# Three stations of a pipelined two-layer decoder divided in two, late halves in other banks, orders written anew

## Chip, cores and metric

One core of a Trainium2 chip runs the kernel. The metric is the device time in microseconds (us), the median of several executions; lower is better. Engines are named as in the profile: PE is TensorE (PEld its weight loads), DVE is VectorE, ACT is ScalarE, POOL is GpSimd, SP is SyncE, whose queue issues every DMA.

## What is computed

Two decoder layers on 32 sequences of 128 rows and 256 channels. Each of the six sublayers is added to its input and normalized over the channels:

```python
x = layernorm(x + L0_attn(x))            # 16 heads, window of 7 rows, learned window weights
x = layernorm(x + L0_xattn(x, ctx))      # cross attention, one head, additive mask
x = layernorm(x + L0_ffn(x))             # 8 experts, each attends over its 16 best rows of a sequence
x = layernorm(x + L1_attn(x))            # attention with a decay mask
x = layernorm(x + L1_xattn(x, ctx))      # argmax picks one context row each; 16 heads over them
x = layernorm(x + L1_ffn(x))             # w1, depthwise conv over rows, silu, w2; ternary weights, int8-like rows
```

## The kernel before, in words

The 32 sequences form 16 groups of two (NG = 16, 256 rows each). A group passes eight **stations**, which are Python generators on each engine: Q queries and A windowed (first attention), B cross (cross attention), X experts, C decayed (decay attention), D choose and E memory (the argmax attention), F feed_forward. S is the setup of weights. A station yields after each step. `ORDER` holds one string for each engine; `walk` reads it letter by letter, and each letter issues the next step of that station on that engine, so the whole interleaving of the groups is written out by hand. While group 15 is in A, group 13 or so is in C and group 11 in F. An engine works strictly in its own order; between engines there are only semaphores.

A step is named here by station, group and number on its engine, counted from 0: PE's C4.5 is the sixth step of C for group 4. The numbering of the undivided station is used for both kernels.

PSUM has eight banks. Station Q and A share bank_a, X has bank_x, F has bank_f, E has the four banks_e, and B, C and D share bank_c. Each PE step fills a bank, ACT or DVE empties it, and the next PE step of the station waits for that: a round trip, which other stations' PE steps have to cover. The stations' PE steps are: X 0 to 5 routing, gather and the experts' projection, X 6 to 12 rotation transposed, scores, softmax, values, projection back; E 0 to 8 scores, maxima, logits, exponentials, values, for two sequences in turn, E 9 and 10 turning the heads and projecting with wc1x; F 0 to 5 quantization rows and the four w1 products, F 6 to 8 the second row scale and the w2 product.

Between two sublayers stands the norm. DVE adds the bank to x (`norm`, L932, instruction at L934, one instruction and one accumulator read for each of the two sequences), ACT squares and sums (`squares`, L1386), POOL works out scale and shift (L1674 to L1680), ACT applies them (`normed`, L1397). The semaphore `added` was raised once, after both sequences:

```python
for b in range(GB):
    last = dve.scalar_tensor_tensor(x[:, b, :], bank[b], ..., accum_out=n.sums[:, b:b + 1])
last.then_inc(n.added, 1)
```

In F, DVE and ACT alternate for each of four pairs of channel blocks (jj): DVE empties the w1 product (`evacuated`, L1310), ACT starts the convolution (`middle`, L1642), DVE adds its two shifted taps (`convolved`, L1319), ACT takes the tanh (L1647), DVE multiplies (`gated`, L1329), ACT takes the magnitude (L1651), DVE keeps the largest (`largest`, L1335). After that come the maximum over channels, a second scale (L1355 to L1361), the scaled copies (L1365), and the w2 product. On DVE the loop was, for every group: largest(at - 3), gated(at - 2), convolved(at - 1), evacuated(at).

Of the kernel before, what the change touches and what calls it, by code (L numbers as in the profile page):

```python
# [11 lines left out]
ALU = mybir.AluOpType  # L12
# [3 lines left out]
P = 128  # L16
# [46 lines left out]

UNIT16 = 2.0 ** 24
# [5 lines left out]
        "QQQASSASASSQBQBAQAADSBABASBBQBQBXXASAXQXAXBXBAAXBBXQBXQXXBXAXAXQCXCABXXBXABAXBQXCXQCXXXBXCAXCAXBXQDAXDXD"  # L70
        "XDADXEABBXXEBQCEBEQEXCXECEXCXECECEXDAXEDADQDAFXDFDFAEBXFBEXBFXBEXEBFBXACXEQCECECXQECFXCXEXDEFXDEXDFDAXAD"
        "FDQEFXBFEBXFBXFBEXEFABCEAXABEXCQCECXQXCECEXFDXFEXEDFXDADFADXDQEFBFXEFBABXEBXFXBFEBAXEACXCEQCXEXCQECFXCXE"
        "DXEFXDAEDXDFDADQEFXBFEFBFXBAXBEFEFXACECAXBBXECQCEXQXCEXFCXEFXEDEXFDXADDFADFDFQEXBFAEBXFBXBXEFBEBAACEXCEX"
        "CQXEXCFEDXCEXCFXEQXEFDXADADFQDFDAEFXBEBXFBXBEXFBEBFACEAXECXQCQCXEXCFXCXDXEXFEDAEDEDFDADXQEFBFEFXBXABFBXB"
        "FXCEFEABXEXCAECQXCXEXFQCXECEFXEDXAEDFDXDADDFEFBFEFXBXBQBFXABEXEBFACEXCAXECECXQXCFECEXDFEXQDXDXAEDFDXDAEF"
        "QBXFEFBFBXBFEXEXFBABAEACXECXQCQECXFXECXECXEXDXAFEDADXDFDQDAEFXBFEFBFXBABXFBEBEXFEACEXQXCECXCXEXCEXECXDFX"
        "EFDQXADFDADXFDQEBFEFBXFBABEFXEXBFBEXCAACEXCECXFXDECXFCEXBEXEDXFDXDFADAFDFXEXBEFBXBFEXBEBFXCXECXECXECXFXC"
        "FECEXEDXEFDXDDFFDFDXFXECXCECFCXECFCEDXEXEDXEXFDXFEXDXDEDEFECECECFFFECEFCCFDFEEDEDEDFEDEFDEFEEFFFEEFEFEFE"
        "EEFEFEFFFFFFFFFFFFF"
    ),  # L80
    "DVE": (
        "QSQSSQQASSSSSASSSASSSSSSSSSAASSSAAASSAAAAAAAAAAAAAAAQQQQSSSSSSSSSSSSASSSSSSSSSAAASSSSSSSBBAASSSSSAAABAAA"
        "AAAAAAAAAAAAQXSSXXXXXXXXAXXQQQAAAXBBXXAAAAABXXAAAAAAAAAAAAAAAQQQQXAAXXXXXXXXXAXAXBBAAAAAXXBXAAAAAAXXAAAC"
        "ACAAAAAQQQQXCAAXXXXXXXXXAXAXDDDXEXXAAEBBXXEEAEEEEAABAAAAAAAAAAAAEEQAAQQQCCAEECXEAAFFFDDDAXAXXXFXXXXEXEFF"
        "FXFEEFXEEEEFFBBFFFXXXBAAFFAAAXFFXFFAAAEEAFAACCFAFAAAFFFCEEAAAAFFFXAQEFQQQFDDDFFFXAXXXAXXXXXEXEFXEEFFFEEE"
        "EFFFFBBFFFFAAXXFXFABEEAFAAAFFXAXAAFAAACCAAFFAACEEFFFAAQFFFFXAEQQQFAAFFFDDDAAXXXXXXXXXEEFXXEEEEEAEFFFBBFF"
        "FFAFXXXFFBFAAXXFFFEEFAAAAAAAAFFCCFAAFAAAACFEEFFAAAXAFFFQEFQQXQDDDXFXXXAXXXXFFFAEEXXEFEFFEEEEFFAFFFBBAFFF"
        "FFXXXFFAAFBAFEAAFXXEAAACCFFAAAAAAAACFFFEEFFFXFAAEAAFQXQQQFFFXDDDXXXAXXXXFAFFEEFAFXEFFFEFEEBBEEXFFFABXXXF"
        "AAFAAAFEFXXFEAAAFAAFFCCFFFAAAAEEAACAAXFFFFAAEQFQQQFFFXADDDXXXXXXXXAAAEEFXXEEFFEEEFFEBBFFFXXXBFFFAFAEFFEX"
        "AAAFFAAAXFFCCFFAAAAACFFFAAAAXAAAEEFFFFQQQEDDDQFAFFFXAXXXEXEXXXXEFXXEFFFFBBEEEAFFFEFFFFAXXXFBFFXFXAAFAAAF"  # L90
        "EEFFAAAACCAAAAFFFAAAACEEAAXAFFFFEQQQFQDDDXFFFXXXXAXXXEEAFXEXXFFFEFEEEBEBFFFAAFFFXXBFXFFFFAFAXEXEFAAAAAAC"
        "CFFAAAFFFCEEAAAAAAAAFFFAXFQQQQEDDDFXXXXXFFFAEEXXXXAXXEFEFFFEEEEBFBFFFFFFFAABXXXAAFFFEFAAAFFEXXFFAAAAAAAC"
        "CFAAAFFAAAEEACAQXQQFFFEFQAAXXXDDDXFFFFXXXXXAAEEXXEFEFFFFBBFEEEEFFFBFFFXXAXAFFFEEFXFFXAAAAAAAFFCCAAAAEEAA"
        "CAAXAFFFAAFFFEFXXXXXXXXQXQFDDDFFFAQQAXXEEEFEFFEEEEFFBBFFFAAFFFXXFXBFFFFAAFAAAEEAAAFXXFCFCAFFFAAAAAACEEFF"
        "FFAAXAAEAFFXFFXDDDXXXXXXAXFXXEEFFEEFFEEEEBBFFFXXXBFFFFXXFFFFEEFFFFCCFFFFFFCEEFXEFXXXXXFFFXDDDXXXFXXFFEFE"
        "FFFEEFEECEECFFFFFFCXXXFFFFXXEEFFFFFFFFFDDDXEEFEEEFFFEEEEEEFCCFFFFFCFFFFFFEEFFFFFFFFDDDFEEFFFFFFEFEEFFFEE"
        "EEEEFFFFFFFFEEFFFFFFFFFFFFEEFFFFFFFEFFFFFFFFFFFFFFFFFFFFFFFFFFFFFFFF"
    ),
# [14 lines left out]
    "POOL": (
        "ABBABBXXABBXCXCABXBCCXEABBXCFCXEFABBXCCFXEFABBXCCFXEFABBXCCXFEFABBXCFCXEFABBXCCFXEFABBXCFCXEFABBXCFCXEFA"
        "BBXCFCXEAFBBXCCXFEFABBXFCCXEFABBXCFCXEFCCXFXFECCFEFFEFFF"
# [47 lines left out]
def build(nc, io, out):  # L163
    ctx = ExitStack()
    with ctx:
# [53 lines left out]
        _, carve = area("area_a", 8216)  # L219
# [54 lines left out]
        am_f, sc1_f, rs1_f, rs2_f = (carve(GB) for _ in range(4))  # L274

# [29 lines left out]
        x_in = [next(sems(f"x_in{i}")) for i in range(2)]  # L305

# [46 lines left out]
        I = w["ident"][:, :]  # L353

# [17 lines left out]
        def _(sp):  # L372
# [77 lines left out]
            def feed_forward(g):  # L450
                sp.wait_ge(n_f.done, g + 1)
                sp.dma_start(out[g * T:(g + 1) * T, :].rearrange("(b t) d -> t b d", b=GB),
                             xs[g % NX][:, :, :]).then_inc(y_out, 16)
                yield
# [7 lines left out]
        def _(pe):  # L462
# [99 lines left out]
            def windowed(g):  # L562
# [33 lines left out]
                until("a", n_a.added, g + 1)  # L596
                yield

            def cross(g):
# [35 lines left out]
                until("c", n_b.added, g + 1)  # L635
                yield

            def experts(g):
                x = xs[g % NX]
                if g:  # L640
                    pe.wait_ge(n_x.added, g)
# [25 lines left out]
                for j in range(EJ):  # L667
# [9 lines left out]
                    yield  # L677
                pe.wait_ge(x_rot, g + 1)
                qkv3 = blocks(qkv_x, EJ)
                for j in range(EJ):  # L680
                    for i in range(2):
                        at = 2 * j + i
                        last = pe.transpose(bank_x[:, at * P:(at + 1) * P], qkv3[:, j, i * HP:(i + 1) * HP], I)
# [1137 lines left out]
```

## Time and profile before

| what | us |
|---|---|
| device time, median of 3 executions (lowest, highest) | 1035.07 (1033.67, 1036.02) |
| device time of the profiled execution | 1034.66 |
| its span in the profile | 1032.9 |
| PE busy | 915.1 (89% of the span) |
| DVE busy | 864.8 (84%) |
| ACT busy | 744.9 (72%) |
| POOL busy | 205.5 (20%) |

The span is what the views are made of; the device time of the same execution is 1.8 us longer. The profile lists for each instruction its start, its length and what ended the idle time before it. PE's mean granted clock over the span is 0.97 of full speed.

### The profile page before, as it was taken

The numbers are of one execution on the slowest core, as the hardware profiler recorded it, in microseconds if no ns is written. First come the engines' busy times: TensorE is split into PE (matmuls) and PEld (weight loads), VectorE is DVE, ScalarE is ACT, GpSimd is POOL, SyncE is SP. The second block draws the span as 40 slices with busy tenths as digits, with TensorE's granted clock in tenths as the row PEclk, the third lists the DMA queues.
The fourth block names the chain that finished last, engine by engine and source line by source line (L and its number), as shares of the span: only waits on it lengthen the run. The fifth ranks groups of instructions, "written<-read, shape, count | busy, mean of one in ns | idle before, by whom it ended". The sixth has DMA issues, their size and how long they took to land.

```text
span 1032.9 us, 20266 instructions
## 1 busy us (share of the span) xinstructions
PE 915.1 (89%) x7382; PEld 666.8 (65%) x7382; DVE 864.8 (84%) x2216; ACT 744.9 (72%) x1857; POOL 205.5 (20%) x469
## 2 busy tenths in 40 slices
PE   6778998999999999999999999999999988897552
PEld 4566666767676776767775767768676756574331
DVE  4987668599898999899999999998999886868755
ACT  2375565777877878787878788777968787867643
POOL 2011221213131211313131312213131312110010
PEclk9989999999999999999999999999999999999765
DMA  8932221110303030211203030302102000000000
GB/s 269 370 80 82 71 61 32 46 47 22 92 1 113 1 112 1 71 42 52 62 11 102 1 92 22 110 3 68 46 31 72 22 1 21 2 22 2 11 10 11
DMA packets 36628, 59.06 MB, mean 57 GB/s; under 512 B 6656, under 2 KB 15872, under 8 KB 36016
## 3 DMA queue, kind: packets, MB, share of 16 engines
q1 hardware_dynamic: 36528, 57.76, 18.1%
q8 instruction: 59, 0.97, 0.4%
q14 instruction: 41, 0.34, 0.1%
HBM read 28.77 MB, written 4.19 MB: 32 GB/s over the span
## 4 chain that ended last, share of the span: by engine, by line
PE 54%; ACT 17%; DVE 16%; SPq 6%; issue 4%; POOL 3%; DMA 1%; ACTq 0%; POOLq 0%; DVEq 0%
PE bank_c L465 16%; PE banks_e L465 8%; PE bank_a L465 7%; PE bank_x L465 6%; DVE area_f L1319 4%; PE bank_f L465 3%; ACT area_e L1608 3%; DVE neg_top L1259 3%; ACT squares_out L1393 3%; SPq L435 2%; PE banks_e L843 2%; ACT area_f L1642 2%; PE bank_a L571 2%; PE bank_x L674 2%; DVE x L934 1%
## 5 line engine op out<-in xcount | busy, mean ns | idle before, releaser
L1319 DVE SCALAR_TENSOR_TENSOR area_f<-area_f,w_convw 128x254 f32<-128x254 f32 x256 | 111.7, 478 | 9.7 <-ACT area_f L1642 7.7
L1381 ACT ACTIVATE area_bx<-bank_x 128x512 f32<-128x512 f32 (+1 forms) x144 | 70.2, 499 | 22.3 <-PE bank_x L674 7.5
L1057 DVE TENSOR_TENSOR area_a<-area_a 128x512 f32<-128x512 f32 x112 | 73.0, 684 | 14.2 <-ACT area_a L1381 12.5
L1259 DVE TENSOR_REDUCE neg_top<-banks_e 128x8 f32<-128x1024 f32 x64 | 76.4, 1219 | 10.1 <-PE banks_e L465 9.9
L1642 ACT ACTIVATE area_f<-area_f,w_convb,w_convw 128x256 f32<-128x256 f32 x128 | 69.8, 595 | 17.8 <-DVE area_f L1310 17.6
L1608 ACT ACTIVATE area_e<-banks_e 128x512 f32<-128x512 f32 x128 | 69.1, 598 | 10.2 <-PE banks_e L843 10.1
L1112 DVE TENSOR_TENSOR area_a<-area_a 128x512 f32<-128x512 f32 x112 | 74.9, 684 | 1.7
L1116 DVE TENSOR_TENSOR area_a<-area_a 128x512 f32<-128x512 f32 x96 | 65.7, 684 | 0.3
L1381 ACT ACTIVATE area_a<-bank_a 128x512 f32<-128x512 f32 (+1 forms) x80 | 44.2, 552 | 26.2 <-PE bank_a L465 21.0
L1381 ACT ACTIVATE area_bx<-bank_c 128x512 f32<-128x512 f32 x64 | 34.7, 542 | 33.7 <-PE bank_c L465 26.3
L465 PE MATMUL bank_x<-area_bx 128*128 128x128 f32 (+1 forms) x256 | 51.6, 334 | 4.1 <-ACT area_bx L1381 3.1
L1688 POOL TENSOR_TENSOR area_bx<-area_bx,minus 128x2 f32<-128x2 f32 x16 | 11.8, 740 | 197.9 <-ACT area_bx L1405 197.9
L1310 DVE TENSOR_TENSOR area_f<-bank_f,area_f 128x512 f32<-128x512 f32 x64 | 43.8, 684 | 7.3 <-PE bank_f L465 6.9
L1647 ACT ACTIVATE area_f<-area_f 128x512 f32<-128x512 f32 x64 | 40.4, 631 | 12.8 <-DVE area_f L1319 12.5
L465 PE MATMUL bank_f<-area_f,w1q 128*128 128x256 f16 x256 | 41.3, 287 | 9.3 <-DVE area_f L1310 7.1
L465 PEld LDWEIGHTS bank_x<-area_bx 128*128 128x128 f32 x256 | 40.7, 190 | 12.8 <-ACT area_bx L1381 6.2
L674 PE MATMUL bank_x<-w_wqkv_e,area_bx 128*32 128x384 f32 x512 | 47.9, 492 | 0.0
L1329 DVE SCALAR_TENSOR_TENSOR area_f<-area_f 128x512 f32<-128x512 f32 x64 | 43.9, 685 | 3.0 <-ACT area_f L1647 2.0
L1381 ACT ACTIVATE area_e<-banks_e 128x256 bf16<-128x256 f32 (+1 forms) x64 | 34.6, 541 | 16.0 <-PE banks_e L496 8.2
L1365 DVE TENSOR_TENSOR area_f<-area_f,bank_f 128x512 f16<-128x512 f32 x64 | 40.2, 681 | 5.3 <-PE bank_f L866 5.2
L465 PE MATMUL banks_e<-chosen_key,chosen_q 32*128 32x256 f32 x512 | 37.6, 408 | 6.6 <-DVE neg_top L1259 4.5
L465 PE MATMUL banks_e<-area_e,chosen_v 128*32 128x512 f32 x256 | 35.3, 618 | 8.6 <-ACT area_e L1608 8.6
(318 smaller groups left out, 2575.1 us busy)
## 6 DMA issues: line engine op xcount, KB each, us to landing
area_a<-area_a SPq DMA_DIRECT2D x96, 224.0 KB
area_a<-in_xT SPq DMA_DIRECT2D x16, 256.0 KB, 2.9
area_bx<-in_ctxT SPq DMA_DIRECT2D x16, 256.0 KB, 3.0
x<-in_x SPq DMA_DIRECT2D x16, 256.0 KB, 3.6
area_d<-in_ctxT SPq DMA_DIRECT2D x16, 256.0 KB, 2.7
y<-x SPq DMA_DIRECT2D x16, 256.0 KB, 2.2
w_wqkv_e<-in_wqkv_e SPq DMA_DIRECT2D x1, 3072.0 KB, 11.2
area_f<-in_raw SPq DMA_DIRECT2D x2, 1024.0 KB, 12.2
```

Source lines behind the costliest of these rows:

```text
L465: last = pe.matmul(out_ap, l, r, start=i == 0 and not opened, stop=closes and i == len(pairs) - 1)
L674: last = pe.matmul(bank_x[ES * q:ES * (q + 1), 0:3 * HP], xgf[:, c, e, :], wq[:, c, e, :], start=c == 0, stop=c == DC - 1)
L1057: return dve.tensor_tensor(product_of(wi).rearrange("p (n t) -> p n t", t=P), qT0.rearrange("p c (b t) -> p (c b) t", t=P), kT0.rearrange( ...
L1112: made[wi] = own.mark(dve.tensor_tensor(v4, v4, bc(e4[:, :, wi, :], 3, DH), ALU.mult))
L1116: added = dve.tensor_tensor(vw[:, to, :], vw[:, to, :], vw[:, wi, :], ALU.add)
L1259: dve.tensor_reduce(top[:, b, r:r + 2, :, 0].rearrange("p r (par c) -> p r c par", c=DC), banks_e[:, r:r + 2, :].rearrange("p r (c par k) ...
L1310: dve.tensor_tensor(blocks(th_f[jj % 3], 2), blocks(bank_f[:, :], 2), bc(tscale_f, 1, 2), ALU.mult).then_inc(f_h, 1)
L1319: last = dve.scalar_tensor_tensor(c4[:, i, :, dst], h4[:, i, :, src], cwt3[:, 2 * jj + i, k:k + 1], c4[:, i, :, dst], ALU.mult, ALU.add)
L1329: dve.scalar_tensor_tensor(c_f[jj], th_f[jj % 3], 1.0, c_f[jj], ALU.add, ALU.mult).then_inc(f_silu, 1)
L1381: return act.activation(dst, src, ACT.Copy)
L1608: act.activation(pT_e[:, r * 4 * P:(r + 1) * 4 * P], bank_e[r][:, :], ACT.Exp, scale=float(DH) ** -0.5).then_inc(e_exp, 1)
L1642: last = act.activation(c4[:, i], h4[:, i], ACT.Identity, bias=w["convb"][:, j:j + 1], scale=cwt3[:, j, 1:2])
```

## The change

**Stations.** X becomes X (steps 0 to 5 on PE) and Y `combine` (6 to 12); E becomes E (0 to 8) and T `connect` (9 and 10); F becomes F (0 to 5) and H `gate` (6 to 8). The other engines' steps are divided in the same places. The work of a group is the same. A second half may now stand in a string behind first steps of the next group's first half.

**Banks.** With `LATE = 13`:

```diff
+        def joined(g):
+            return (bank_a, bank_a) if LATE <= g < NG - 1 else (bank_e[0], bank_e[2])
+        def upper(g):
+            return bank_a if g == NG - 2 else bank_x
+        def gating(g):
+            return gate_late if g == NG - 2 else gate_f
+        def rear(g):
+            return bank_x if LATE <= g < NG - 1 else bank_f
```

So T of groups 13 and 14 uses bank_a, Y of group 14 bank_a, H of groups 13 and 14 bank_x, and F of group 14 has its own buffers (in the area of A, which is done by then). PE's waits follow, among them:

```diff
             def memory(g):
...
+                elif g <= LATE:
+                    pe.wait_ge(n_e.added, GB * g)
                 else:
-                    pe.wait_ge(n_e.added, g)
+                    pe.wait_ge(e_att, 2 * g)
...
             def feed_forward(g):
...
-                if g:
-                    pe.wait_ge(n_f.added, g)
+                if g > LATE:
+                    pe.wait_ge(f_h, NJ * g)
+                elif g:
+                    pe.wait_ge(n_f.added, GB * g)
```

The w2 product of group 15 goes to bank_a and bank_x instead of bank_a and bank_c.

**Norm.** `added` is raised for each sequence, and ACT's squares wait for their own:

```diff
                 for b in range(GB):
-                    last = dve.scalar_tensor_tensor(x[:, b, :], bank[b], ...)
-                last.then_inc(n.added, 1)
+                    dve.scalar_tensor_tensor(x[:, b, :], bank[b], ...).then_inc(n.added, 1)
...
-                act.wait_ge(n.added, g + 1)
                 for b in range(GB):
+                    act.wait_ge(n.added, GB * g + b + 1)
```

**Last group.** Of the last norm ACT applies one sequence and DVE the other; the last store waits for both:

```diff
+                if g == NG - 1:
+                    dve.wait_ge(n_f.scaled, n_f.steps * NG)
+                    dve.tensor_scalar(x[:, 1, :], x[:, 1, :], n_f.scale[:, 0, 1:2], n_f.scale[:, 1, 1:2],
+                                      ALU.mult, ALU.add).then_inc(last_normed, 1)
```

In F of group 15 the loops turn round: DVE takes evacuated(at), convolved(at - 1), gated(at - 2), largest(at - 3), and ACT

```diff
-                for at in range(NJ + 3):
-                    for lag, step in ((3, magnitude), (2, tanh), (1, middle)):
+                lags = ((0, middle), (2, magnitude), (1, tanh)) if g == NG - 1 else ((3, magnitude), (2, tanh), (1, middle))
```

**Orders.** The strings of PE, DVE, ACT and POOL are written anew, SP's is the same. The last of PE's characters, before and after:

```diff
-...EEDEDEDFEDEFDEFEEFFFEEFEFEFEEEFEFEFFFFFFFFFFFFF
+...DEDEDEDHETDHDTHEEFFFEEFEFEFEEEHTHTHFFFFFFHHHHHH
```

and of ACT's:

```diff
-...EFFFFEFEEEEFFEFFFFEEFFEEFFEFEEFEFFFFFFFFFFFFFFFFFF
+...HFFFHEFEEEEFFFEFFFEEFFEEFFEFTTTFFFFFFFFFFFFFFFHHHH
```

As another place, the steps between C4.5 and D4.1. On PE:

```diff
-C4.5 X5.11 E3.8 D4.0 X5.12 E3.9 F2.7 X6.0 D4.1
+C4.5 X5.11 D4.0 E3.8 X5.12 D4.1
```

and on ACT, around the squares C4.5 and the norm C4.6 (X5.10 is the pair at L1542, X5.9 a copy of bank_x):

```diff
-C4.4 X5.9 X5.10 C4.5 D4.0 C4.6
+C4.4 E3.10 X5.9 C4.5 X5.10 D4.0 C4.6
```

At the start of DVE's string S0.0 to S0.2 now stand before Q0.0, and X0.0 to X0.8 before Q2.0.

## Rows read from the trace of the kernel before

**Rows 1.** Windows: us, busy us per engine (instructions), granted clock, DMA share, GB/s.

```profile
231.00:770.00 539.00, 517.64 (x4331) 386.02 (x4331) 495.84 (x1279) 424.26 (x1078) 125.30 (x272) 1.00 0.16 50
770.00:950.00 180.00, 158.39 (x1375) 112.94 (x1373) 144.74 (x369) 144.16 (x357) 32.39 (x79) 1.00 0.08 23
...
960.00:988.00 28.00, 17.67 (x136) 8.88 (x136) 21.27 (x46) 17.58 (x35) 0.76 (x3) 0.69 0.03 10
...
1000.00:1033.00 33.00, 8.85 (x36) 4.50 (x36) 18.60 (x39) 11.71 (x23) 1.55 (x5) 0.55 0.03 9
```

**Rows 2.** Waits of PE, 231 to 950 us: total us, times, longest.

```profile
PE bank_x L465 <- ACT area_bx L1381: 3.6, 7, 1.4
...
PE bank_c L496 <- ACT x L1400: 0.9, 2, 0.6
```

**Rows 3.** Timeline of PE, last stretch: start, us, instruction, idle before.

```profile
917.16 1.89 PE L465 MATMUL banks_e<-w_wc1x,area_e 128*128 128x256 f32 x8
...
920.01 1.15 PE L465 MATMUL banks_e<-chosen_key,chosen_q 32*128 32x256 f32 x16 [0.53 <-DVE x L934]
...
960.75 2.09 PE L465 MATMUL banks_e<-chosen_key,chosen_q 32*128 32x256 f32 x16 [2.54 <-DVE neg_top L1259]
...
988.35 3.40 PE L465 MATMUL banks_e<-w_wc1x,area_e 128*128 128x256 f32 x8
...
1002.30 1.04 PE L465 MATMUL bank_f<-area_f,w1q 128*128 128x256 f16 x4 [0.79 <-DVE area_f L1310]
```

**Rows 4.** Timeline of POOL at the hand-over from memory attention to feed-forward.

```profile
994.89 0.20 POOL L1680 TENSOR_TENSOR bn_scale_e<-bn_negmean_e,bn_scale_e 128x2 f32<-128x2 f32 x1
```

**Rows 5.** Timeline of ACT, the same hand-over and the end.

```profile
996.01 0.58 ACT L1400 ACTIVATE x<-x,bn_scale_e 128x256 f32<-128x256 f32 x1
...
997.97 0.89 ACT L1625 ACTIVATE area_f<-x,area_f 128x256 f16<-128x256 f32 x2
...
1026.76 0.51 ACT L1393 ACTIVATE squares_out<-x,bn_sums_f 128x256 bf16<-128x256 f32 x1 [8.86 <-DVE x L934]
...
1029.72 0.58 ACT L1400 ACTIVATE x<-x,bn_scale_f 128x256 f32<-128x256 f32 x1
```

**Rows 6.** Timeline of DVE, last group.

```profile
991.79 0.42 DVE L934 SCALAR_TENSOR_TENSOR x<-banks_e,x 128x256 f32<-128x256 f32 x1 [0.99 <-PE banks_e L465]
...
997.64 0.21 DVE L1302 TENSOR_SCALAR area_f<-area_f,wmean 128x2 f32<-128x2 f32 x1
1001.56 0.69 DVE L1310 TENSOR_TENSOR area_f<-bank_f,area_f 128x512 f32<-128x512 f32 x1 [3.71 <-PE bank_f L465]
1003.41 1.79 DVE L1319 SCALAR_TENSOR_TENSOR area_f<-area_f,w_convw 128x254 f32<-128x254 f32 x4 [1.16 <-ACT area_f L1642]
...
1018.66 0.43 DVE L1352 TENSOR_TENSOR area_f<-area_f 128x256 f32<-128x256 f32 x1
...
1021.54 2.48 DVE L1365 TENSOR_TENSOR area_f<-area_f,bank_f 128x512 f16<-128x512 f32 x4 [0.78 <-PE bank_f L866]
1025.76 0.48 DVE L934 SCALAR_TENSOR_TENSOR x<-bank_a,area_f,x 128x256 f32<-128x256 f32 x1 [1.75 <-PE bank_c L912]
```

**Rows 7.** One line, L1040: ns min/median/max.

```profile
L1040 DVE TENSOR_SCALAR w_vp<-w_vp x2: 346/350/354, 50.6 to 50.9; 128x255 f32<-128x255 f32 x2
```

**Rows 8.** Timeline of PE, group 4 from the decayed to the choosing station.

```profile
351.90 1.03 PE L465 MATMUL bank_c<-v_c,area_c 128*128 128x256 f32 x4
...
358.75 0.65 PE L496 MATMUL bank_c<-w_ident,x 128*128 128x128 f32 x4
```

**Rows 9.** Timeline of ACT, the same microseconds.

```profile
354.00 0.84 ACT L1542 ACTIVATE area_bx<-bank_x,area_bx 128x256 f32<-128x256 f32 x2 [1.30 <-PE bank_x L465]
354.73 0.51 ACT L1393 ACTIVATE squares_out<-x,bn_sums_c 128x256 bf16<-128x256 f32 x1
...
358.11 0.59 ACT L1400 ACTIVATE x<-x,bn_scale_c 128x256 f32<-128x256 f32 x1
```

**Rows 10.** Timeline of the SP queue at the start.

```profile
45.83 8.61 SPq L435 DMA_DIRECT2D area_a<-area_a  x12
```

More of the change, by code:

```diff
@@ L274, in build @@
         am_f, sc1_f, rs1_f, rs2_f = (carve(GB) for _ in range(4))
+        gate_f = (c_f, top_f, am_f, sc1_f, rs1_f, rs2_f)
+        _, carve = area_a, second
+        gate_late = ([carve(W2) for _ in range(NJ)], carve(W2), *(carve(GB) for _ in range(4)))
         bits = area_e[:, 0:15 * P]
@@ L1211, in experts @@
                 dve.wait_ge(x_spread, g + 1)
-                norm(n_x, x, halved(bank_x))
+                norm(n_x, x, halved(bank))
                 yield
@@ L1337, in feed_forward @@
                 top_step = [0]
-                for at in range(NJ + 3):
+                for at in range(NJ + 3 if g == NG - 1 else 0):
+                    if at < NJ:
+                        evacuated(at)
+                        yield
+                    if 0 <= at - 1 < NJ:
+                        yield from convolved(at - 1)
+                        yield
+                    if 0 <= at - 2 < NJ:
+                        gated(at - 2)
+                        yield
+                    if 1 <= at - 3:
+                        largest(at - 3)
+                        yield
+                for at in range(0 if g == NG - 1 else NJ + 3):
                     if 1 <= at - 3:
@@ L1398, in normed @@
                 act.wait_ge(n.scaled, n.steps * (g + 1))
-                act.activation(x[:, 0, :], x[:, 0, :], ACT.Identity, scale=n.scale[:, 0, 0:1], bias=n.scale[:, 1, 0:1])
-                act.activation(x[:, 1, :], x[:, 1, :], ACT.Identity, scale=n.scale[:, 0, 1:2],
-                               bias=n.scale[:, 1, 1:2]).then_inc(n.done, 1)
+                for b in range(1 if n is n_f and g == NG - 1 else GB):
+                    last = act.activation(x[:, b, :], x[:, b, :], ACT.Identity, scale=n.scale[:, 0, b:b + 1],
+                                          bias=n.scale[:, 1, b:b + 1])
+                last.then_inc(n.done, 1)
             def exponentials(s, negmax, sums):
@@ L1541, in experts @@
                 for j in range(EJ):
-                    last = act.activation(up_x[:, j * D:(j + 1) * D], bank_x[:, j * D:(j + 1) * D], ACT.Copy,
+                    last = act.activation(up_x[:, j * D:(j + 1) * D], bank[:, j * D:(j + 1) * D], ACT.Copy,
                                           scale=sums_x[:, j:j + 1])
@@ L1661, in feed_forward @@
                 yield
[L1663 removed]
+            walk(ORDER["ACT"], {"H": gate, "Y": combine, "T": connect, "S": setup, "Q": queries, "A": windowed, "B": cross, "X": experts, "C": decayed, "D": choose, "E": memory, "F": feed_forward})
         @block.gpsimd
@@ L1734, in _ @@
             last.then_inc(setup_pool, 1)
-            walk(ORDER["POOL"], {"A": windowed, "B": cross, "X": experts, "C": decayed, "E": memory, "F": feed_forward})
+            walk(ORDER["POOL"], {"A": windowed, "B": cross, "Y": combine, "C": decayed, "T": connect, "H": gate})
 def constants():
```

232 lines of the change are left out of this document (147 added, 85 removed).

## The prediction

> **What bounds the kernel now.** I read the busy time by stretch first [rows 1]. From 231 to 770 us PE is busy for 517.6 of 539 us at the full clock, so 21.4 us, or 4%, are idle: there PE's work sets the time, and only gaps between its steps can be won. From 770 to 950 us 21.6 of 180 us are idle; at 4% it would be 7.1, so some 14.5 us are excess. After 950 us the engines mostly wait for one another: from 960 to 988 us PE is busy for 17.7 of 28 us, from 1000 to 1033 us for 8.9 of 33. That end is one chain, memory attention and then feed-forward of group 15.
>
> The waits of PE come next [rows 2]: no wait is large. The copies of bank_x cost it 3.6 us in seven waits between 231 and 950 us, the wait for the normed rows ahead of D1 0.9 us in two. The timelines of the end show which of those waits lie on the chain [rows 3 to 6].
>
> **What the change does, part by part.** No engine gains or loses work, but for one instruction of 256 columns that goes from ACT to DVE.
>
> *The division itself.* I followed the letters of both strings. On PE no Y, T or H step stands behind a step of the next group's X, E or F: in spite of the spare banks, PE keeps the sequence that it had. On DVE H's norm stands behind first steps of F in two groups (8 and 14), on ACT the norm of X or F stands behind such steps in most groups. The banks therefore only take waits away, and those are few. Cost and gain in the steady stretch: 0 from the banks.
>
> *Start of E14.* PE waited 0.53 us for DVE's norm of group 13 before the scores of E14, at 920.01 [rows 3]. Now those scores wait for e_att, which was raised earlier, since T13 works in bank_a. The scores and the 2.4 us of maxima behind them move ahead by the same 0.53: **-0.5**. Late next is PE's own queue (C15.1 stands behind it).
>
> *Hand-over of group 15 from E to F.* DVE's norm starts at 991.79. The increment for each sequence lets ACT begin its squares after the first half, 0.35 to 0.4 us sooner. POOL had shift and scale ready at 995.09 (994.89 + 0.20) [rows 4], but ACT applied them until 996.59, which is 996.01 + 0.58 [rows 5], because squares of F14 stood in between; without them it could have started at 995.1 and ended 1.1 later, at 996.2. The new string has T's three steps together and F14's squares and norm at the very end. So the rows are normed near 996.2 - 0.4 = 995.8, 0.8 sooner. After that ACT ran the norm of F14 and only then, at 997.97, the scaled copies of F15 [rows 5]; in the new order nothing stands between. DVE had the scale just before L1302 started, that is 1.05 us after the normed rows (996.59 to 997.64) [rows 6], so the copies can start at 995.8 + 1.1 = 996.9, against 997.97. I take **-1.0**, which holds the 0.8. F14's norm moves behind F15's first DVE steps and falls into the 3.7 us in which DVE waited ahead of 1001.56 [rows 6]; its squares and store fall into ACT's 8.9 idle us before 1026.76 [rows 5]. If that cover went, they would cost some 2 us. Two of DVE's four scaled copies of F14 now stand behind T15's norm, which waits for PE; the w2 product of F14 then ends near 996, just ahead of F15's first PE step. No cost, 1 us of slack.
>
> *F15's loop.* Before, DVE went from 1001.56 to 1018.66 with the largest [rows 6], 17.1 us, of which 1.16 us waited for ACT's middle in front of the first convolution. A convolution takes 1.79 us; four instructions of 512 columns take 2.48 us in a row, at 1021.54 [rows 6], so some 0.6 each. Its work there is 4 x 0.6 (evacuated) + 4 x 1.75 + 4 x 0.6 (gated) + 3 x 0.6 (largest) = 13.6 us. The new loop empties the second product in that first wait, once PE's product of 1.04 us, at 1002.30, is there [rows 3]. Going through the new sequence with the same durations, I find DVE waiting once more than hoped, since ACT's magnitude(at - 2) now stands ahead of tanh(at - 1) and itself waits for gated: the largest is done near 1017.7. **-0.95**; at best the whole of the waits, 17.1 - 13.6 - 1.1 for the first product = 2.4, at worst 0.
>
> *The end.* The squares of the last norm start at 1026.76, after DVE's second half; they can start after the first, 0.45 sooner [rows 5, 6]. ACT then took 1.1 us for both sequences, ending 1030.3 (1029.72 + 0.58) [rows 5]. Now ACT takes one, 0.6, and DVE the other; the nearest row for that is a scale and shift-like TENSOR_SCALAR of 255 columns, 0.35 us [rows 7]. Minus 0.5. **-0.9** together; at worst, if the second semaphore on the store adds its own hop, -0.7.
>
> *Start.* The SP queue is issuing without a break up to 54.5 us (the last twelve shifts from 45.83, 8.61 us) [rows 10] and its order stays. DVE now takes S0.0 to S0.2 before Q0.0 and hands the first products over by perhaps 0.5 us later; SP hides that. X0 ahead of Q2.0 may bring 0.3 before the third round of shifts. I take 0 and keep -0.7 to +0.7.
>
> Sum: -0.5 - 1.0 - 0.95 - 0.9 = -3.35 us. The profiled execution took 1034.66, which gives 1031.3; it lies 0.4 below the median of the runs, which gives **1031.7**. Elsewhere the orders differ by a few places per group; with nothing in the traces to say which is denser, I take 0, and the rivals carry it.
>
> **Rivals.**
>
> *A norm's round trip uncovered (slower).* The first half of D for a group needs C's normed rows, and PE waits for them in its queue. In group 4 the old string had 358.75 - 352.93 = 5.8 us between C4.5 and D4.1 [rows 8], eight steps without a wait at D4.1; ACT's norm ended at 358.70 (358.11 + 0.59) [rows 9], so it was just in time. The new string has four steps there, some 4.35 us. If the trip stays, PE waits 1.4 us, and the same holds for groups 3 and 9 (my count of the steps gives 4.7 against 7.4, and 4.7 against 5.5); five more groups come down to 4.3 to 5.8, at about 0.5 each. That is 3 x 1.4 + 5 x 0.5 = 6.7 us, and 1031.7 + 6.7 = **1038.4**. Against it: ACT's squares of C4 waited behind the pair of X5.10 (354.00, 0.84) and started at 354.73 [rows 9]; the new string puts them ahead, and the increment by sequence gives up to 0.4 more, so the trip can shrink by 1.1 and PE would wait 0.3. It decides from a loss of 5.5 us on, that is when the trips of those eight groups stay within 0.2 us of what they were.
>
> *Wider cover in X and the late groups (faster).* By the same count the new strings put more PE work into the narrowest round trips: 2.7 us instead of 1.7 on average between X6 and X7, 2.2 instead of 1.4 between X8 and X9. That can take the 3.6 us of waits for bank_x's copies [rows 2] and a part of the 14.5 us of excess from 770 to 950 us. A quarter of that and two thirds of the 3.6 are 6 us: **1025.7**. For it: the squares moved as above show that ACT's order was adapted to PE's. Against it: the PE string after 860 us differs from the old one in few places.
>
> *The clock at the end (faster).* From 960 to 988 us the granted clock is 0.69, from 1000 on 0.55, between the levels 1.2 and 2.4 GHz, after PE had idled ahead of it [rows 1]. The scores of E15 took 2.09 us at 960.75, those of E14 1.15 at 920.01, the wc1x product 3.40 at 988.35 against 1.89 at 917.16 [rows 3]. If the half-microsecond that E14 gains moves PE's work closer together and the clock stays up until 992, these two alone give 2.5 us, and the logits and values between them about as much: -5 us, **1026.7**. The Trainium skill (TensorE: Matmul & The Clock Gate, Part 1: The HAM clock gate) says that the reduced clock is the default state and that activity releases it. By that rule a tail with the same idle stretches, which PE's unchanged last steps make likely, keeps its slow matmuls; this is why the chance is small.
>
> *The change does nothing (same).* The last 36 steps of PE's string are the same as before, and PE never uses the new freedom. If ACT's queue or the clock's phase gives back what the end gains, as 1 to 3 us can go in any stretch, the time is **1034.5**.
>
> **How the numbers follow.** A difference of 0.2%, 2.1 us, is about what a measurement of this kernel can tell from none. The forecast gets 0.42 (its own range, 1029.5 to 1034; 0.36 of it faster, 0.06 same), the wider cover 0.16, the clock 0.06, nothing 0.14, the uncovered trips 0.22 (0.02 of it same). Faster 0.36 + 0.16 + 0.06 = 0.58, same 0.06 + 0.14 + 0.02 = 0.22, slower 0.20. The range 1024.5 to 1038.5 goes from below the faster rivals to the price of the slower one.
>
> **What the profile after would show.** Right: between 231 and 770 us some 21 us idle; no wait for DVE's L934 before E14's scores; ACT's squares 0.4 us before DVE's second half is read out; the scaled copies of F15 4.8 to 5.2 us after T15's norm starts, not 6.2; 16 us instead of 17.1 in DVE's F15; 4.1 instead of 5.1 us from DVE's last norm to the end of the last applied rows. Wrong: PE waiting before D1 for ACT's normed x by more than 3 us in all, or a steady stretch whose idle differs by more than 4 us, or another clock from 957 to 992 us.

## The result, and the profile after

| | before | after |
|---|---|---|
| device time, median (lowest, highest) | 1035.55 (1033.67, 1038.33) | 1019.40 (1019.00, 1020.11) |
| profiled execution: device time, span | 1034.66, 1032.9 | 1020.11, 1018.3 |
| PE, DVE, ACT busy | 915.1, 864.8, 744.9 | 915.2, 858.8, 738.6 |

The ratio is 0.9843, with a 95% interval from 0.9823 to 0.9863: 16 us faster, where 1031.7 was forecast and 1024.5 was the lowest end of the range. The direction was right; the size and its place were not.

The same PE instruction marks the same progress in both traces, so I cut both spans at three of them: the first memory scores of group 0 (start of the instruction at 157.59 us before, 158.73 after), the w2 product of group 11 (867.56 and 857.28), the first memory scores of group 15 (957.06 and 945.23).

| stretch | before | after | difference |
|---|---|---|---|
| start to the scores of E0 | 157.6 | 158.7 | +1.1 |
| to the w2 product of group 11 (steady) | 710.0 | 698.6 | -11.4 |
| to the first scores of E15 | 89.5 | 87.9 | -1.6 |
| to the end | 75.8 | 73.1 | -2.7 |

Between the first two marks the windows read as follows (columns as in [rows 1]), before:

```profile
157.59:867.56 709.97, 675.61 (x5673) 500.56 (x5670) 636.61 (x1632) 555.66 (x1414) 158.41 (x347) 1.00 0.15 46
```

and after, followed by the fixed windows that answer to [rows 1]:

```profile
158.73:857.28 698.55, 673.09 (x5673) 501.41 (x5670) 631.84 (x1632) 553.39 (x1416) 157.57 (x347) 1.00 0.15 47
...
231.00:770.00 539.00, 523.06 (x4390) 392.69 (x4377) 498.08 (x1291) 428.50 (x1097) 125.10 (x275) 1.00 0.17 51
770.00:950.00 180.00, 157.18 (x1381) 113.27 (x1384) 148.41 (x385) 141.18 (x358) 35.26 (x85) 1.00 0.06 19
960.00:988.00 28.00, 17.19 (x103) 9.44 (x104) 18.41 (x45) 15.37 (x32) 1.71 (x6) 0.72 0.00 1
988.00:1018.00 30.00, 8.92 (x36) 4.37 (x34) 18.69 (x40) 12.70 (x27) 2.63 (x8) 0.50 0.05 18
```

In the steady stretch PE's idle time fell from 34.4 to 25.5 us, and that is where most of the time came from: many small gaps. Its busy total is 2.5 us less for the same instructions. That total counts overlapping instructions once, their ends are modelled, and their durations added singly are equal within 0.5 us, so how the 11.4 us divide into idle and busy time is not certain. The stretch from 770 to 950 us, which I took for the place with 14.5 us to win, holds 22.8 us of idle time now against 21.6.

The end came out as drawn. DVE and ACT, after (start, us, instruction, idle before):

```profile
979.96 0.42 DVE L989 SCALAR_TENSOR_TENSOR x<-banks_e,x 128x256 f32<-128x256 f32 x1 [2.19 <-PE banks_e L492]
...
988.94 0.69 DVE L1381 TENSOR_TENSOR area_f<-bank_f,area_f 128x512 f32<-128x512 f32 x1 [2.79 <-PE bank_f L492]
...
1004.78 0.43 DVE L1436 TENSOR_TENSOR area_f<-area_f 128x256 f32<-128x256 f32 x1
...
1012.10 0.48 DVE L989 SCALAR_TENSOR_TENSOR x<-bank_a,area_f,x 128x256 f32<-128x256 f32 x1 [1.96 <-PE bank_x L967]
...
1015.14 0.41 DVE L1461 TENSOR_SCALAR x<-x,bn_scale_f 128x256 f32<-128x256 f32 x1 [2.15 <-POOL bn_scale_f L1789]
```

```profile
980.48 0.51 ACT L1486 ACTIVATE squares_out<-x,bn_sums_e 128x256 bf16<-128x256 f32 x1 [4.03 <-DVE x L989]
...
985.26 0.91 ACT L1729 ACTIVATE area_f<-x,area_f 128x256 f16<-128x256 f32 x2 [1.24 <-DVE area_f L1370]
...
1012.69 0.51 ACT L1486 ACTIVATE squares_out<-x,bn_sums_f 128x256 bf16<-128x256 f32 x1 [5.24 <-DVE x L989]
...
1015.14 0.60 ACT L1493 ACTIVATE x<-x,bn_scale_f 128x256 f32<-128x256 f32 x1 [1.36 <-POOL bn_scale_f L1789]
```

The scaled copies of F15 start 5.30 us after T15's norm (6.18 before), the loop of F15 lasts 15.84 us on DVE from 988.94 to 1004.78 (17.1 before), and from the last norm to the last applied row it is 3.64 us (4.54 before).

### The profile page after: what moved, and what is told of

Read it like the earlier page. It is cut to its first block, busy times and chain, and to the rows that moved or that the text cites. A ratio compares the mean times of both kernels' runs of the same rounds, so it can differ in the third digit from the quotient of the medians.

```text
span 1018.3 us, 20308 instructions
## 1 busy us (share of the span) xinstructions
PE 915.2 (90%) x7382; PEld 669.6 (66%) x7382; DVE 858.8 (84%) x2217; ACT 738.6 (73%) x1856; POOL 209.2 (21%) x469
## 4 chain that ended last, share of the span: by engine, by line
PE 59%; ACT 17%; DVE 16%; issue 3%; POOL 2%; SPq 2%; DMA 1%; DVEq 0%; POOLq 0%; ACTq 0%
PE bank_c L492 17%; PE banks_e L492 8%; PE bank_a L492 7%; PE bank_x L492 6%; PE bank_f L492 4%; PE bank_x L703 3%; ACT area_e L1707 3%; PE bank_a L598 2%; DVE area_f L1390 2%; ACT area_bx L1474 2%; ACT squares_out L1486 2%; PE banks_e L878 2%; DVE neg_top L1316 2%; ACT x L1493 2%; PE bank_c L523 2%
## 5 line engine op out<-in xcount | busy, mean ns | idle before, releaser
L1390 DVE SCALAR_TENSOR_TENSOR area_f<-area_f,w_convw 128x254 f32<-128x254 f32 x240 | 104.7, 478 | 3.7 <-ACT area_f L1746 2.1
L1474 ACT ACTIVATE area_bx<-bank_x 128x512 f32<-128x512 f32 (+1 forms) x140 | 68.2, 500 | 21.6 <-PE bank_x L703 7.0
L1746 ACT ACTIVATE area_f<-area_f,w_convb,w_convw 128x256 f32<-128x256 f32 x120 | 65.4, 595 | 9.6 <-DVE area_f L1381 9.6
L1474 ACT ACTIVATE area_a<-bank_a 128x512 f32<-128x512 f32 (+1 forms) x80 | 44.1, 551 | 31.2 <-PE bank_a L492 22.8
L1474 ACT ACTIVATE area_bx<-bank_c 128x512 f32<-128x512 f32 x64 | 34.4, 537 | 28.7 <-PE bank_c L492 17.3
L492 PE MATMUL bank_x<-area_bx 128*128 128x128 f32 (+1 forms) x240 | 48.2, 334 | 2.1 <-ACT area_bx L1474 1.9
L492 PEld LDWEIGHTS bank_x<-area_bx 128*128 128x128 f32 x240 | 38.3, 191 | 11.4 <-ACT area_bx L1474 7.4
L1400 DVE SCALAR_TENSOR_TENSOR area_f<-area_f 128x512 f32<-128x512 f32 x60 | 41.2, 686 | 2.6 <-ACT area_f L1751 1.8
L1751 ACT ACTIVATE area_f<-area_f 128x512 f32<-128x512 f32 x60 | 37.8, 630 | 7.6 <-DVE area_f L1390 7.5
L1757 ACT ACTIVATE area_f<-area_f 128x512 f32<-128x512 f32 x60 | 37.8, 631 | 6.4 <-DVE area_f L1400 6.3
L1474 ACT ACTIVATE area_e<-banks_e 128x512 f32<-128x512 f32 (+1 forms) x62 | 33.4, 539 | 11.3 <-PE banks_e L523 6.1
```

Of the source, the lines that this page charges most:

```text
L492: last = pe.matmul(out_ap, l, r, start=i == 0 and not opened, stop=closes and i == len(pairs) - 1)
L1390: last = dve.scalar_tensor_tensor(c4[:, i, :, dst], h4[:, i, :, src], cwt3[:, 2 * jj + i, k:k + 1], c4[:, i, :, dst], ALU.mult, ALU.add)
L1400: dve.scalar_tensor_tensor(c_f[jj], th_f[jj % 3], 1.0, c_f[jj], ALU.add, ALU.mult).then_inc(f_silu, 1)
L1474: return act.activation(dst, src, ACT.Copy)
L1746: last = act.activation(c4[:, i], h4[:, i], ACT.Identity, bias=w["convb"][:, j:j + 1], scale=cwt3[:, j, 1:2])
```

## The experiments

The medians below stand against 1019.4 (and 1018.9 when it ran again). The kernel before, timed beside them on four occasions, had medians from 1035.75 to 1036.61, and 1035.55 beside the changed kernel: 1 us between medians of different occasions says nothing by itself. Where a term is smaller than the spread of runs, I read it from the milestones of the profiles: in the steady stretch they repeat to 0.1 us.

**The orders taken back.** All four strings of the kernel before, each letter written as its half; the code stays. The first letters of PE:

```diff
-"QQQASSAASSQBQQBSAQAADSBABASBBQBQXBXASAXQXAXABXBABYBYQBYYQYYBAYAXQCXCABXXBAXBAXBQYCYQ...
+"QQQASSASASSQBQBAQAADSBABASBBQBQBXXASAXQXAXBXBAAYBBYQBYQYYBYAYAXQCXCABXXBXABAXBQYCYQ...
```

> The code of the changed kernel (divided stations, banks, norm counts by halves, the last group's loops and last norm) with the order strings of the kernel before, each letter written as that of its half. Theory 'orders' (the 11.4 us that the stretch from 159 to 858 us lost come from where the strings now put the steps): the steady stretch is back at about 710 us, the end keeps most of its 2.8, so about 1031.5 us (1029.5 to 1033). Rival 'code' (the squares that no longer wait for both sequences, the waits and banks): 1020 to 1024 us, with the steady stretch below 703.

Measured 1032.16 us (1028.59 to 1033.40). Its steady stretch is 709.5 us, 0.5 less than in the kernel before and 10.9 more than after. Behind it, 161.9 us are left to the end against 165.3 before and 161.0 after. So the new code under old strings is worth 0.5 us in the steady stretch and 3.4 behind it; the orders are worth 10.9 in the steady stretch and 0.9 behind it. Idle time of PE ahead of its groups of instructions in the steady stretch (last column: us, and what ended it), under the old strings:

```profile
L492 PE MATMUL banks_e<-chosen_key,chosen_q 32*128 32x256 f32 x416 | 29.8, 400 | 3.0 <-DVE neg_top L1316 1.3 <-ACT chosen_v L1474 1.3
L523 PE MATMUL bank_c<-w_ident,x 128*128 128x128 f32 x152 | 23.5, 277 | 1.9 <-ACT area_bx L1474 1.3 <-DVE x L989 0.5
L598 PE MATMUL bank_a<-area_a,w_headsum 128*32 128x256 f32 x308 | 23.4, 384 | 1.8 <-DVE area_a L1111 1.8
L528 PE MATMUL banks_e<-w_ident,area_e 128*128 128x128 f32 x104 | 16.1, 277 | 2.3 <-ACT area_e L1474 2.2
L492 PE MATMUL bank_c<-area_d,chosen_q 128*128 128x128 f32 x96 | 13.3, 281 | 1.8 <-ACT chosen_q L1474 1.5
L502 PE MATMUL bank_c<-bias_parts,ones_bf 128*128 128x512 bf16 x25 | 9.6, 384 | 2.1 <-ACT area_c L1656 1.8
```

and under the new ones:

```profile
L492 PE MATMUL banks_e<-chosen_key,chosen_q 32*128 32x256 f32 x416 | 29.8, 400 | 1.8 <-ACT chosen_v L1474 1.0 <-DVE neg_top L1316 0.2
L523 PE MATMUL bank_c<-w_ident,x 128*128 128x128 f32 x152 | 23.8, 279 | 3.2 <-DVE x L989 1.2 <-ACT area_bx L1474 1.2 <-ACT x L1493 0.7
L598 PE MATMUL bank_a<-area_a,w_headsum 128*32 128x256 f32 x308 | 23.4, 384 | 0.1
L528 PE MATMUL banks_e<-w_ident,area_e 128*128 128x128 f32 x104 | 16.0, 276 | 0.9 <-ACT area_e L1474 0.9
L492 PE MATMUL bank_c<-area_d,chosen_q 128*128 128x128 f32 x96 | 13.2, 281 | 0.6 <-ACT chosen_q L1474 0.3
L502 PE MATMUL bank_c<-bias_parts,ones_bf 128*128 128x512 bf16 x25 | 9.7, 386 | 0.7 <-ACT area_c L1656 0.3
```

Counts are equal and durations nearly so; only the last column differs. Five of the six groups lose 1.2 to 1.7 us each. They belong to four stations (A, C, D, E), none to X, and the norms' transposes (the second row) wait more than under the old strings. No one wait carries the gain. The strings of all engines were always exchanged together, so which engine's string brings it is not shown.

**Old strings up to group 8.**

```diff
 at the cut, PE (before it all as in the kernel before):
-... B7.1 X6.3 B7.2 F3.3 X6.4 A8.0 ...
+... F3.3 X6.3 B7.2 X6.4 A8.0 ...
```

> The changed kernel with the strings of the kernel before up to the first step of the windowed station of group 8 (at about 370 us) and the new ones behind it. Theory 'bit by bit': the gain of the new strings is made in every part of the steady stretch and kept from there; the run with all old strings was 4.5 us further behind at 370 us than at 141 us, so this one stays those 4.5 us behind to the end: about 1023.5 us (1022.5 to 1024.5), with milestones behind 400 us at a constant distance from the changed kernel's. Rival 'one lead': the gain comes from a state that the start sets up or that only the whole string keeps: 1028 or more, or below 1020.5.

Measured 1024.47 us (1022.45 to 1029.94), ratio to the kernel before 0.9896, interval 0.9873 to 0.9919. Against the changed kernel its profile stands at -1.7 us at 141 us, +3.8 at 535 us, and +3.8 at every milestone from there to 945: 5.5 us lost in the first half, none after. So the gain of the first half is kept, and the second half makes its own. It isn't even: with all strings old, the lag behind the changed kernel, counted from the scores of E0, is 5.1 us at 368 us, 2.6 at 477 and 10.9 at the w2 product of group 11.

**The start.** The same cut at group 3.

> The changed kernel with the strings of the kernel before up to the first step of the windowed station of group 3, and the new ones behind it. Theory: the start of the changed kernel is 1.1 us late (milestones at 158 us), since the second raw load on SP waits for TensorE's set-up step, which was moved back; with the old start this is given back and 1018.0 to 1018.7 us come out. Rival: what is early at 158 us waits later for the engines with more to do, 1019.2 to 1019.6 us.

Measured 1019.83 us (1017.87 to 1022.08): no difference to be seen, the theory missed. The scores of E0, at 158.7 us in the changed kernel's first profile, came at 160.6 us in the profile of the same kernel run again and at 157.9 to 160.2 in seven others that share its start; with the old start they came at 157.1 to 160.7 in four profiles. The 1.1 us that I read as lost are within what the start does by itself.

**The division's freedom.** In 19 places ACT's string uses it, in two DVE's: the last step of a group's norm stands behind the next group's first steps. Three kernels undo this, in 14, 16 and 18 of ACT's places and in one of DVE's. The first puts the last step forward to where the next group begins. The second puts both side by side at a later place, so that the next group's first steps go back. The third does as the first, and as the second only where the first had left the place alone (the experts of groups 3, 6, 8 and 11); the feed-forward of group 14 is all that it leaves. On ACT in groups 5 and 8 (X5.12 and X8.12 are norms, X6.0 and X9.0 copies that PE waits for):

```diff
 group 5, first and third kernel
-D4.2 X6.0 E3.12 X5.12 A7.2
+D4.2 X5.12 X6.0 E3.12 A7.2
 group 5, second kernel
+D4.2 E3.12 X5.12 X6.0 A7.2
 group 8, second and third kernel (as it was in the first)
-X9.0 A10.2 D7.2 E6.12 D7.3 E6.13 F5.15 X9.1 A10.3 ... F6.2 X8.12
+A10.2 D7.2 E6.12 D7.3 E6.13 F5.15 A10.3 X8.12 X9.0 X9.1 ... F6.2
```

(the third has A10.3 behind X9.1.)

> The changed kernel with 15 of the 19 places undone where ScalarE (and once VectorE) begins a station's next group before the old one's last step: there the last step of the old group goes ahead again. Theory 'freedom' (the division pays because a norm's last step may lie behind the next group's first copies): each place gives a wait of 0.3 to 1 us back, 1024 to 1031 us. Rival 'any order' (the gain is in orders that the undivided stations allowed as well): within 1.5 us of 1019.4.

Measured 1033.91 us (1032.40 to 1036.10).

> The changed kernel with 17 of the 19 places undone where a station's next group begins on ScalarE (once on VectorE) ahead of the old one's last step, each time by putting both side by side at the latest place at which the order still runs through: the old group's last step moves up by at most 7 steps (3 for the late groups 12 and 13). Groups 1 (experts) and 10 (feed-forward) are left. The first such run put the last steps up by as many as 18 and cost 14 us, nearly all of it at four of those far moves, and 0.1 us in the groups 5 to 9. Theory 'any order': the division's freedom itself is worth little, 1019.5 to 1022 us. Rival 'freedom': 1025 to 1031 us.

Measured 1077.07 us (1073.91 to 1078.76).

> The changed kernel with all overlaps but one (feed-forward of group 14) undone on ScalarE and VectorE, so that up to there its strings are ones that undivided stations could run: the old group's last steps go ahead of the next group's first ones, and for the experts of groups 3, 6, 8 and 11, where that alone deadlocks, both stand side by side at the first place that runs through (3, 3, 6 and 2 steps behind). The run without these four took 1033.9 us; where the first copies of the next group went back instead of the last step forward, the six places cost 3 to 13 us each. Theory 'freedom': these four cost 2 to 5 us each, 1042 to 1054 us, so that the new strings without the division are worse than the old ones (1032.2). Rival 'any order': they cost 0.1 us as in the groups 5, 7 and 9, 1034 to 1036 us.

Measured 1058.24 us (1055.98 to 1058.92). The first lost its time at the far moves, by its milestones: 3.9 us at the experts of group 1 (18 steps), 3.2 from there to 337 us, 6.9 after 697 us, and 0.2 between 337 and 697, where the norms of groups 5, 7 and 9 went ahead by 2 to 6 steps; there the freedom isn't worth anything. At the experts of groups 3, 6, 8 and 11 it is: they put the third kernel another 2.7, 6.7, 7.0 and 7.2 us back. That is 23.6 us, near the difference of the two medians (24.3), and more than either theory gave. The second kernel lies 46 us above the higher of its two theories. PE's waits in the third kernel (total, times, longest) in its steady stretch of 732.4 us, and the idle time ahead of the routing product:

```profile
PE bank_x L492 <- ACT area_bx L1474: 22.8, 11, 6.1
...
L492 PE MATMUL bank_x<-area_bx,wr_pad 128*32 128x128 f32 x192 | 9.3, 314 | 21.3 <-ACT area_bx L1474 21.2
```

The changed kernel waits there 1.1 us in all; the second kernel, which puts the copies back the farthest, has 39.0. PE's string sends X(g+1).1, the routing product, soon after X(g+1).0, and what stands between them is ACT's copy. With an undivided station on ACT this copy is locked behind X(g).12, a norm that has to wait for DVE and POOL, and PE, which works in order, stands still. So my rival "any order" fell: these strings need the divided stations. Whether other strings would do as well for undivided stations wasn't tried, so how much of the 10.9 us needs the division stays open: the old strings, which undivided stations can run, take 1032 us, less than the third kernel's 1058.

**Squares that wait for both sequences**, with the new strings and with the old ones:

```diff
-                for b in range(GB):
-                    act.wait_ge(n.added, GB * g + b + 1)
+                act.wait_ge(n.added, GB * (g + 1))
+                for b in range(GB):
```

> The changed kernel, but ScalarE starts a norm's two squares only when VectorE has added both sequences. Theory 'orders': nobody waits for most norms, so the time rises only by what the last norms cost, 0.3 to 1.0 us: 1019.7 to 1020.4. Rival 'code': the norms of all groups lie in somebody's wait; one addition of 0.4 us for each of 5 norms in 14 groups is 28 us of lag, of which a third would count: 1025 or more.

Measured 1025.07 us (1023.67 to 1025.82); the steady stretch is 702.6 us, 4.0 more than after, and the ratio to the kernel before (0.9880 against 0.9843) says 3.8. My theory, 1020.4 at most, missed by 4.7 us. Where in PE's string the 4.0 us arise is only in part visible: it waits 1.4 us instead of 0.7 for normed rows ahead of D1 and its like, and no other wait grew by more than 0.6. The rival's "1025 or more" holds, but the profile of the next run speaks against its reason, a worth of every norm's addition.

> The changed code with the old strings and whole squares: ScalarE's squares wait for both sequences, as in the kernel before. With the new strings whole squares cost 5.7 us (4.0 of it in the stretch from 159 to 858 us). Theory 'fitted': the new strings are drawn up for the shorter norm and the old ones for the longer one, so here it costs 0.3 to 1.5 us: 1032.4 to 1033.7. Rival 'same worth': 1035 to 1038.

Measured 1032.61 us (1030.31 to 1037.57), the steady stretch 709.4 us against 709.5 with halved squares. So by the profiles the earlier squares are worth nothing under the old strings and 4.0 us under the new ones: the strings seem drawn closer around the shorter trip. Code and order then don't add up; the 10.9 us of the orders hold those 4.0. This rests on one profile of each kernel, and the whole times don't confirm it: the ratios to the kernel before, timed beside each, are 0.9982 (0.9967 to 0.9998) with whole squares and 0.9946 (0.9926 to 0.9967) with halved ones, 3.7 us apart, and the profiled execution with whole squares was the fastest of its twelve.

**The late groups' banks**, the same kernel on two occasions:

```diff
-LATE = 13
+LATE = 15
```

> The changed kernel with the late groups' memory-attention and feed-forward second stations in their own banks again (the start of the late groups set to 15, which none reaches; the experts of group 14 keep their other bank). The prediction costed the banks at 0. Theory: within 0.5 us, 1019.0 to 1019.9, since TensorE's order leaves time between a bank's users. Rival: the stretch from 857 to 988 us, where these stations stand closer, gets the 1.5 us back that it lost: 1020.5 to 1021.5.

Measured 1022.15 us (1020.22 to 1024.09).

> The kernel with the late groups' second stations in their own banks once more. Its first runs had a median 3.2 us above the changed kernel's of that call, but its profile only 0.7 us less any difference of the start, in the stretch from 857 us on. Theory: 0.5 to 1 us slower than the changed kernel, 1019.9 to 1020.5. Rival: 3 us slower, 1022 to 1022.5, for a reason that one profile does not show.

Measured 1022.00 us (1020.70 to 1023.14). Its steady stretch is 698.6 us as in the changed kernel; the loss lies behind it, in two waits. PE in this kernel, at the scores of E14 and at the first step of F15:

```profile
910.32 1.15 PE L492 MATMUL banks_e<-chosen_key,chosen_q 32*128 32x256 f32 x16 [0.53 <-DVE x L989]
...
988.46 0.66 PE L908 MATMUL bank_f<-w_ident,area_f 128*128 128x128 f32 x2 [1.64 <-DVE x L989]
```

and in the changed kernel:

```profile
908.21 1.15 PE L492 MATMUL banks_e<-chosen_key,chosen_q 32*128 32x256 f32 x16
...
985.40 0.69 PE L908 MATMUL bank_f<-w_ident,area_f 128*128 128x128 f32 x2 [0.59 <-DVE area_f L1371]
```

The 0.53 us of [rows 3] are back, and F15 waits 1.05 us longer, now for the addition of F14's norm, which still reads bank_f. That makes 1.6 us; in the first occasion's profile the stretch behind the steady one is only 0.7 us longer. The medians say 2.6 to 3.2, where 0.5 at most was expected; the rest I can't place. The 1.05 us are no gain over the kernel before, where the same step waited for DVE's scale, 3.5 us after that addition:

```profile
997.90 0.57 PE L866 MATMUL bank_f<-w_ident,area_f 128*128 128x128 f32 x2 [4.41 <-DVE area_f L1302]
```

They are what the new order would have cost with the old bank.

**The loop of F15 as before.**

```diff
-                for at in range(NJ + 3 if g == NG - 1 else 0):
+                for at in range(0):
...
-                lags = ((0, middle), (2, magnitude), (1, tanh)) if g == NG - 1 else ((3, magnitude), (2, tanh), (1, middle))
+                lags = ((3, magnitude), (2, tanh), (1, middle))
```

> The changed kernel with the last group's feed-forward loop in the old order of its steps on VectorE and ScalarE (lags 3, 2, 1). The prediction costed the new loop at 0.95 us and the loop measured 15.84 us against 17.1. Theory: 0.9 to 1.4 us slower, 1020.3 to 1020.8 us, all of it between the first copy of the last group's loop and its last maximum. Rival: the new place of the steps beside the loop (the feed-forward of group 14 in the idle time of ScalarE) does it, and the loop's order nothing: 1019.2 to 1019.7.

Measured 1020.49 us (1019.39 to 1021.26). DVE's first copy out of the bank and the maximum behind the loop:

```profile
988.83 0.69 DVE L1381 TENSOR_TENSOR area_f<-bank_f,area_f 128x512 f32<-128x512 f32 x1 [1.97 <-PE bank_f L492]
...
1005.92 0.42 DVE L1436 TENSOR_TENSOR area_f<-area_f 128x256 f32<-128x256 f32 x1
```

17.09 us, as in the kernel before, against 15.84: the order of the loop is worth 1.25 us.

**The last norm on ACT alone.**

```diff
-                for b in range(1 if n is n_f and g == NG - 1 else GB):
+                for b in range(GB):
```

(and without DVE's half and the second wait of the store.)

> The changed kernel with both halves of the very last norm on ScalarE, as before. The theory puts one ScalarE step of 0.36 to 0.6 us back on the path and takes a hand-over to the store away: 0.3 to 0.5 us slower, 1019.7 to 1019.9. Rival: VectorE's half is not what the store waits for, no difference.

Measured 1020.06 us (1018.64 to 1020.92). In its profile ACT takes both halves in 1.09 us in the place of 0.60; that and the store's start put 0.5 us between the start of the last w2 instructions and the end (7.38 against 6.89 us). The medians agree with it but can't prove it.

**Tanh ahead of the magnitude**, twice, and the changed kernel beside the second:

```diff
-                lags = ((0, middle), (2, magnitude), (1, tanh)) if g == NG - 1 else ...
+                lags = ((0, middle), (1, tanh), (2, magnitude)) if g == NG - 1 else ...
```

> The changed kernel with tanh ahead of the magnitude in the last group's loop on ScalarE (lags 0 middle, 1 tanh, 2 magnitude). In the trace VectorE waits in the loop for ScalarE's tanh behind a magnitude of 0.5 to 0.6 us that nobody wants yet. Theory: the loop gets 0.3 to 0.8 us shorter, 1018.6 to 1019.1. Rival: the magnitude is late for the running maximum instead, and the loop is as long or longer, 1019.4 to 1020.

Measured 1019.19 us (1018.53 to 1019.82).

> The kernel with tanh ahead of the magnitude in the last group's loop once more, beside the changed kernel of the same call. Its first profile had the loop 1.33 us shorter, of which 0.6 us was a faster clock at the loop's first transposes and products. Theory: 0.7 us less than the changed kernel of this call. Rival: what the loop gains is taken back by the clock, within 0.3 us of it.

> The changed kernel once more, beside the others of this call: 1019.0 to 1020.1 us, the stretch from group 0's first memory scores to group 12's (159 to 858 us) 698.6 us long to 0.3, and the start within 2 us of 159.1.

Measured 1019.48 us (1018.11 to 1020.54, and one execution of 2093.62 that nothing explains) against 1018.94 (1015.98 to 1020.86) for the changed kernel. The loop is 0.7 us shorter in both pairs of profiles (15.15 against 15.84, 14.80 against 15.51), yet the times can't be told apart. It is no proven improvement; I found no version that beats the changed kernel. (In the expectation of the kernel run again, the mark at 858 us is group 11's w2 product, not a score of group 12.)

## Why the prediction was wrong

**The step that failed is the term 0 for the orders elsewhere.** I wrote that they "differ by a few places per group; with nothing in the traces to say which is denser, I take 0". They are worth 10.9 us in the steady stretch. I had looked at the largest waits of PE and found them small; the gain lies in 34.4 us of small waits, 8.9 of which went. (The prediction's own sign of being wrong, a steady stretch whose idle differs by more than 4 us, came true: from 231 to 770 us it is 15.9 us instead of 21.4.) The profile gave the bound: 34.4 idle us in the steady stretch, all of it open to a new order. The range should have reached a good part of it down.

**The division at nothing** failed too. I saw that PE's string never passes its old sequence, wrote "0 from the banks", and gave no other term to the division. What it carries is on ACT, where I saw the overlap in most groups and priced it at nothing: without it, and with these strings, PE waits 20 us more for the copies ahead of the routing product. And of the 1.6 us that the late banks carry by the profile I had the 0.5 of E14; the 1.05 at F15, which with bank_f still held waits for F14's addition, is what they spare the new order. I had written "No cost, 1 us of slack" of F14's w2 product here, and not asked what F15's first step would wait for with the old banks.

**The halved norm** I priced only in the last group. It is worth 4.0 us more in the steady stretch under the new strings; under the old ones one profile shows nothing and the whole times leave it open.

The terms I did work out held. Start of E14: forecast 0.5, and the 0.53 us came back when the banks were undone. Hand-over: 1.0 forecast, 0.9 measured. Loop: 0.95 and 1.25; two profiles of the changed kernel differ by as much as the rest (15.84 and 15.51). End: 0.9 and 0.9, of which about 0.5 is DVE's half; the 5.1 us that the prediction gave for that stretch before are misread, its rows give 4.54. (It also counted eight PE steps between C4.5 and D4.1 where there are seven; the 5.8 us come from the trace and stand.)

That 1032.16 was measured with the old strings, near the forecast 1031.7, is luck in part. By the profiles the code brings 3.9 us there, the sum forecast 3.35; but of the hand-over's 1.0 only 0.4 comes with the code, since ACT still squares and norms F14 in between. T15's norm on DVE and the scaled copies of F15 under the old strings, 5.78 us apart:

```profile
992.75 0.42 DVE L989 SCALAR_TENSOR_TENSOR x<-banks_e,x 128x256 f32<-128x256 f32 x1 [0.82 <-PE banks_e L492]
...
998.53 0.89 ACT L1729 ACTIVATE area_f<-x,area_f 128x256 f16<-128x256 f32 x2
```

The other half comes with the new order.

Start: 0, and no run shows otherwise in time. That SP would hide a later hand-over was not borne out: its last twelve shifts were issued at 47.06 against 45.83 us [rows 10], at 46.1 to 47.2 in nine profiles with the new start and at 45.6 to 46.5 in five with the old one. That is 0.8 us later on average; whether it reaches the scores of E0 can't be told from their spread.

**The rivals.** The uncovered norm trip fell: PE waits for ACT's normed rows ahead of D1 and its like 0.7 us in three waits, 0.9 before [rows 2]. That ACT's earlier squares shrank the trip, as the argument against it said, agrees with the 1.4 us under whole squares. The wider cover in X had the right sign and a wrong place. The waits for bank_x's copies fell from 3.6 to 2.4 us, but 0.6 us of them moved with group 14's to bank_a, which makes 3.0; under the old strings and the new code they are 1.5 and 1.6, together 3.1. So the new order hardly touched them. The two lines of PE's waits from 231 to 950 us that answer to [rows 2]:

```profile
PE bank_x L492 <- ACT area_bx L1474: 2.4, 4, 1.1
...
PE bank_c L523 <- ACT x L1493: 0.7, 3, 0.3
```

The clock at the end did not rise: 0.72 and 0.50 in the windows above, the scores of E15 at 2.09 us and the wc1x product at 3.41, as in [rows 3]:

```profile
948.92 2.09 PE L492 MATMUL banks_e<-chosen_key,chosen_q 32*128 32x256 f32 x16 [2.55 <-DVE neg_top L1316]
...
976.50 3.41 PE L492 MATMUL banks_e<-w_wc1x,area_e 128*128 128x256 f32 x8
```

PE idled 2.55 us ahead of those scores, as before. By the rule of the Trainium skill that the prediction cited (TensorE: Matmul & The Clock Gate, Part 1: The HAM clock gate), a tail with the same idle stretches keeps its slow matmuls; the trace agrees.

## What to carry to other kernels

Where an engine is busy 95% of the steady time and works in a written order, bound a rewritten order by the whole idle time of that engine in the stretch, not by its largest waits. A division of a stage can be worth nothing on the engine that bounds and much on the one that feeds it: look for the copy that the bound engine waits for and ask what stands locked ahead of it. And an order fitted to one latency can make that latency worth more than it was (4.0 us against nothing here, by one profile each); price code and order together.

## What the runs showed of the hardware

In the steady stretch two executions of one program, on different occasions, keep every milestone from 124 to 952 us to 0.1 us of a constant distance, while the start before it differed by 1.8 us and the loop of F15 by 0.33 (15.84 and 15.51). The latter goes with the clock: the second w1 product of F15 took 1.04 us in the one and 0.70 in the other. And a stall costs more than itself: in the third kernel of the freedom, with waits of up to 6.1 us, the granted clock of the steady stretch was 0.98 instead of 1.00, the routing product took 314 ns on average instead of 279, and PE's busy total was 681.7 us instead of 673.1 for the same instructions.
